# Four key tiles of the value product in parts, and two cosine products taken from PSUM by VectorE

## The chip, the cores and the metric

The kernel runs on one core of one Trainium2 chip. The metric is the device time in microseconds (us) of one execution, as the median of several runs; lower is better.

## The reference

A transformer block on four sequences of 1024 tokens with 256 channels: layer norm, then attention with 16 heads of 128 and rotary positions, and beside it a feed-forward net with weights rounded to four bits, both added to the input. All of it is computed in fp32.

```
xn = layernorm(x)
q, k, v = split(einsum('bsd,od->bso', xn, w_qkv))      # 16 heads of 128
q, k = x * cos + rotate_half(x) * sin                  # for each of the two
attn = softmax(q k^T / sqrt(128))                      # 1024 x 1024 for each head
x = x + (attn v) w_out^T + mxfp4_ffn(xn)
```

## The kernel before

**Tiling.** Attention takes the bulk of the time. It goes through 32 pairs of heads (8 pairs for each of four sequences). A pair is eight chunks of work, and a chunk is 256 query rows of one head against its 1024 keys. Chunks are numbered 0 to 7 within a pair here (0 to 15 within a round of two pairs, `k` in the code); `c` counts them through the whole run, 256 in all. There is one step of the program for each chunk. TensorE (PE) does in step k: the scores of the next chunk (two halves of a step, each a query tile of 128 rows against 1024 keys, six matmuls), the projection of a part of q, k or v for the next pair (the places `slot(0)` and `slot(1)`, not filled in every step), the output product of chunk k-2 (`output`, tile `w_ps`) and the value product of chunk k-1 (`values`, tile `o_ps`).

**Parts.** A product that must be exact is done either in fp32, or as three matmuls on numbers split in a high part (fp32r, the rounded copy) and a low part (the difference): high by high, high by low, low by high. The scores, the projections and the output product use parts. In the value product two of the eight key tiles are in parts (`SPLIT = 2`, lines 1296 to 1300) and six are in fp32 (line 1304).

**The way of a chunk.** ACT (ScalarE) turns scores into probabilities with an exponential (line 755) after DVE (VectorE) has found the row maxima (933). DVE transposes them in blocks (943, twice a chunk), the DMA queue of SyncE (SP) moves them to `keys_first` (420, eight DMAs a chunk), ACT makes the high parts of the split tiles (`probs_high`, 761, kept in `seq_parts`), GpSimd (POOL) makes the low parts (`probs_low`, 605), and PE multiplies. ACT (767) and DVE (963, `o_lo`) then split the result for the output product, and DVE adds that to `y` (974).

**Rotations.** Each pair has eight halves of q and k to rotate, m = 0 to 7: `qk0` has 0 to 3, `qk1` has 4 to 7. For each, ACT copies the projection from PSUM (735, and 736 and 737 for the two swapped halves; semaphore `rope_in`), POOL multiplies by cosine (584) and by sine (585) and adds (587; `rotated_sum`), ACT makes the high part (747, `rotated_high`) and POOL the low part (598, `rotated_low`). The buffers `rope_a` and `rope_b` hold two rotations, so the copy for m waits until the low part of m-2 is made.

**What sets the order.** No scheduler: each engine runs its own list in order, written in the functions called `step`. On ACT, `rotated_high` of m=0, 1, 2 stands at the end of steps 3, 4, 5, that of m=3 in the middle of step 6, those of m=4 and 5 at the end of steps 7 and 0, and `probs_high` comes last in each step. On POOL, `probs_low` of the chunk before comes first in each step, and the low part and the sum of the rotations after it. On SP, `move_tile` sends a half chunk once DVE has transposed it. In the first sequence POOL and ACT also split the weights of the next pair (612, 618, 705, 713); later these are loaded.

**Numbers that matter to the change.** `V_SPLIT` lists the v projections whose tiles get parts (`v_low` on DVE, 957). It follows from `SPLIT`.

## Time and profile before

| | us |
|---|---|
| median of 3 runs | 2454.54 (2453.13 to 2455.77) |
| the profiled execution | 2453.68 |
| its span | 2451.9 |
| PE busy | 2417.3 (99% of the span) |
| DVE busy | 1920.8 (78%) |
| POOL busy | 1731.7 (71%) |
| ACT busy | 1678.6 (68%) |

The span runs from the first to the last instruction; the profiled execution is 1.8 us longer than its span. The granted clock of TensorE is at 2.4 GHz throughout (0.999 of it on average). Busy time says how much work an engine has. Whether an engine that is not the busiest can still set the time is seen from the order of its work against that of the others, instruction by instruction.

### The profile page before, as it was taken

How to read it: one execution, taken by the hardware profiler on the slowest of the kernel's cores; microseconds unless marked ns; L12 is line 12 of the kernel's file. 1: busy time of each engine (PE TensorE's matmuls, PEld its weight loads, DVE VectorE, ACT ScalarE, POOL GpSimd, SP SyncE). 2: the span in 40 equal slices, each digit the busy share in tenths (PEclk: the TensorE clock that was granted, in tenths of full speed). 3: DMA queues.
4: the chain of work that ended last, by engine and by line, in shares of the span. 5: the costliest groups of instructions: out<-in, count | busy, mean ns of one | idle time of the engine just before them, and what ended most of it. 6: DMA issues, size and time to landing. Idle time of an engine off the chain costs nothing. (4 is left out here: it accounts for less than half of the span.)

```text
span 2451.9 us, 42811 instructions
## 1 busy us (share of the span) xinstructions
PE 2417.3 (99%) x13168; PEld 2123.8 (87%) x13168; DVE 1920.8 (78%) x2671; ACT 1678.6 (68%) x3039; POOL 1731.7 (71%) x1358
## 2 busy tenths in 40 slices
PE   6999999999999999999999999999999999999999
PEld 5888888888888888888888888888888888888798
DVE  7878888787877877787787778778777877777776
ACT  7777777776776777676677767667776766777433
POOL 4778877777777777777677777777777777777331
PEclk9999999999999999999999999999999999999999
DMA  4666666667666656667666666667676666656832
GB/s 143 181 170 167 169 158 177 158 167 195 183 161 150 156 148 162 156 151 195 180 159 147 164 154 152 162 149 190 158 183 156 151 162 149 156 146 171 240 132 69
DMA packets 400878, 396.72 MB, mean 162 GB/s; under 512 B 38656, under 2 KB 383104, under 8 KB 400768
## 3 DMA queue, kind: packets, MB, share of 16 engines
q1 hardware_dynamic: 400768, 395.67, 62.9%
q14 instruction: 91, 0.75, 0.1%
q8 instruction: 19, 0.31, 0.1%
HBM read 91.43 MB, written 35.65 MB: 52 GB/s over the span
## 5 line engine op out<-in xcount | busy, mean ns | idle before, releaser
L933 DVE TENSOR_REDUCE neg_max<-s_ps 128x1 f32<-128x1024 f32 x512 | 621.1, 1219 | 289.1 <-PE s_ps L1222 288.2
L1222 PE MATMUL s_ps<-seq_parts 128*128 128x512 f32 x3072 | 826.3, 408 | 1.3 <-DVE seq_parts L1097 0.8
L755 ACT ACTIVATE probs<-s_ps,neg_max 128x1024 f32<-128x1024 f32 x512 | 571.1, 1115 | 369.0 <-DVE neg_max L933 365.3
L1304 PE MATMUL o_ps<-keys_first,v_rows 128*128 128x256 f32 x3072 | 706.5, 380 | 1.3 <-ACT v_rows L722 1.3
L943 DVE STREAM_TRANSPOSE turned_blocks<-probs 128x1024 f32<-128x1024 f32 x512 | 630.6, 1237 | 61.3 <-ACT probs L755 38.8
L1222 PEld LDWEIGHTS s_ps<-seq_parts 128*128 128x128 f32 x3072 | 571.5, 188 | 116.9 <-ACT probs L755 1.4
L1304 PEld LDWEIGHTS o_ps<-keys_first,v_rows 128*128 128x128 f32 x3072 | 566.3, 190 | 68.1 <-ACT v_rows L722 1.5
L605 POOL TENSOR_TENSOR keys_first<-keys_first,seq_parts 128x512 fp32r<-128x512 f32 x256 | 333.0, 1301 | 318.1 <-ACT seq_parts L761 318.0
L584 POOL TENSOR_TENSOR rope_a<-rope_a,cos 128x512 f32<-128x512 f32 x252 | 325.7, 1292 | 178.8 <-ACT rope_b L737 178.6
L598 POOL TENSOR_TENSOR seq_parts<-rope_a,seq_parts 128x512 fp32r<-128x512 f32 x252 | 360.2, 1430 | 92.8 <-ACT seq_parts L747 92.8
L1222 PE MATMUL slot_ps<-seq_parts,w_parts 128*128 128x512 f32 x1506 | 387.9, 393 | 0.0
L587 POOL TENSOR_TENSOR rope_a<-rope_a,rope_b 128x512 f32<-128x512 f32 x252 | 326.0, 1294 | 19.8
L585 POOL TENSOR_TENSOR rope_b<-rope_b,sin 128x512 f32<-128x512 f32 x252 | 326.7, 1297 | 0.0
L1222 PEld LDWEIGHTS slot_ps<-seq_parts,w_parts 128*128 128x128 f32 x1506 | 272.9, 189 | 51.7 <-ACT rope_b L737 0.5
L747 ACT ACTIVATE seq_parts<-rope_a 128x512 fp32r<-128x512 f32 x252 | 222.1, 881 | 80.4 <-POOL rope_a L587 79.9
L974 DVE SCALAR_TENSOR_TENSOR y<-w_ps,inv_sum,y 128x256 f32<-128x256 f32 x512 | 224.4, 480 | 33.5 <-DVE inv_sum L951 7.8
L767 ACT ACTIVATE o_hi<-o_ps 128x256 fp32r<-128x256 f32 x256 | 98.0, 383 | 165.5 <-PE o_ps L1304 141.9
L1222 PEld LDWEIGHTS slot_ps<-w_parts,seq_parts 128*128 128x128 f32 x1524 | 197.5, 189 | 9.1 <-issue 0.9
L1222 PE MATMUL slot_ps<-w_parts,seq_parts 128*128 128x256 f32 x1524 | 203.1, 283 | 0.5 <-ACT rope_b L737 0.5
L1222 PEld LDWEIGHTS w_ps<-wo_parts,o_hi 128*128 128x128 f32 x1024 | 175.1, 190 | 29.5 <-DVE o_lo L963 9.1
L1222 PE MATMUL w_ps<-wo_parts,o_hi 128*128 128x256 f32 x1024 | 194.3, 282 | 6.4 <-DVE o_lo L963 6.3
L761 ACT ACTIVATE seq_parts<-keys_first 128x512 fp32r<-128x512 f32 x256 | 159.7, 624 | 59.3 <-DMA keys_first<-turned_blocks 57.8
(118 smaller groups left out, 2606.8 us busy)
## 6 DMA issues: line engine op xcount, KB each, us to landing
keys_first<-turned_blocks SPq DMA_DIRECT2D x2048, 128.0 KB, 2.7
w_parts<-w_qkv_parts SPq DMA_DIRECT2D x72, 512.0 KB, 4.2
w_qkv_parts<-w_parts SPq DMA_DIRECT2D x24, 512.0 KB, 3.7
wo_parts<-w_out_parts SPq DMA_DIRECT2D x48, 256.0 KB, 3.2
seq_parts<-xnt_parts SPq DMA_DIRECT2D x16, 512.0 KB, 4.4
w_raw<-in_w_qkv SPq DMA_DIRECT2D x24, 256.0 KB, 4.1
seq_parts<-xnt_parts SPq DMA_DIRECT2D x6, 1024.0 KB, 8.3
y<-in_x SPq DMA_DIRECT2D x16, 256.0 KB, 3.2
```

The lines of the kernel that those rows point to most:

```text
L584: nc.gpsimd.tensor_tensor(a, a, cos[:, cols], ALU.mult).then_inc(rope_mult, 1)
L585: nc.gpsimd.tensor_tensor(b, b, sin[:, cols], ALU.mult).then_inc(rope_mult, 1)
L587: nc.gpsimd.tensor_tensor(a, a, b, ALU.add).then_inc(rope_sum, 1)
L598: nc.gpsimd.tensor_tensor(lo, total, hi.bitcast(F32), ALU.subtract).then_inc(qk_ready, 1)
L605: nc.gpsimd.tensor_tensor(low, low.bitcast(F32), p_hi[:, slot, :, :, :].bitcast(F32), ALU.subtract).then_inc(p_lo_ready, 1)
L747: nc.scalar.activation(hi, total, ACT.Copy).then_inc(rope_hi, 1)
L755: nc.scalar.activation(probs[:, k2 % 4, :], s_ps[k2 % 2][:, :], ACT.Exp, bias=neg_max[:, col:col + 1], accum_out=row_sum[:, col:col + 1]). ...
L933: nc.vector.tensor_reduce(neg_max[:, k2 % 16:k2 % 16 + 1], s_ps[k2 % 2][:, :], AXX, ALU.max, negate=True).then_inc(max_ready, 1)
L943: nc.vector.transpose(turned_blocks[:, k % 2, n].rearrange("p b j q -> p j b q"), probs[:, (2 * k + n) % 4, :].rearrange("p (j b q) -> p j ...
L974: last = nc.vector.scalar_tensor_tensor(rows, w_ps[:, n * DIM:(n + 1) * DIM], inv_sum[:, col:col + 1], rows, ALU.mult, ALU.add)
L1222: ins = nc.tensor.matmul(out, w, m, start=(n == 0), stop=(n == len(terms) - 1))
L1304: last = nc.tensor.matmul(out, v_rows[:, parity, kt - SPLIT, cols], keys_first[:, slot, :, kt, :].bitcast(F32), start=False, stop=(kt == B ...
```

## The change

- `SPLIT` goes from 2 to 4: four key tiles of each value product are done in three fp32r matmuls each, four in fp32. The high parts of a chunk's probabilities are one ACT copy of 1024 columns in place of 512. The low parts are two POOL subtractions of 512 columns (`FRONT`, tiles 0 and 1; `BACK`, tiles 2 and 3), with a semaphore each, both waited for by PE before the low parts' matmuls. One more v projection in each pair gets a low part from DVE, in step 5.
- For m = 6 and 7 (`FROM_BANK`), ACT no longer copies the projection to `rope_a`, and POOL no longer multiplies it by the cosine: DVE takes it from PSUM, scales it and multiplies it by the cosine in one instruction (`rotated_product`). That stands in DVE's steps 0 (m=6) and 1 (m=7), behind the row maxima and ahead of the reciprocal, the sum to `y` and the transpose. It waits for ACT's two half copies (`rope_in`). POOL's sum and PE's next use of the bank wait for it.
- In step 2 POOL makes the low part of m=7 ahead of the low parts of chunk 1, and ACT its high part ahead of the exponentials.

```diff
-SPLIT = 2
+FRONT_TILES, SPLIT = 2, 4
...
+        FROM_BANK = (6, 7)
...
                 pool.wait_ge(rope_in, p * 8 + m + 1)
-                nc.gpsimd.tensor_tensor(a, a, cos[:, cols], ALU.mult).then_inc(rope_mult, 1)
+                if m in FROM_BANK:
+                    pool.wait_ge(rope_product, p * len(FROM_BANK) + FROM_BANK.index(m) + 1)
+                else:
+                    nc.gpsimd.tensor_tensor(a, a, cos[:, cols], ALU.mult).then_inc(rope_mult, 1)
...
-                low = keys_first[:, slot, :, 0:SPLIT, :]
-                nc.gpsimd.tensor_tensor(low, low.bitcast(F32), p_hi[:, slot, :, :, :].bitcast(F32),
-                                        ALU.subtract).then_inc(p_lo_ready, 1)
+                low = keys_first[:, slot, :, FRONT, :]
+                nc.gpsimd.tensor_tensor(low, low.bitcast(F32), p_hi[:, slot, :, FRONT, :].bitcast(F32),
+                                        ALU.subtract).then_inc(p_lo_front, 1)
+                low = keys_first[:, slot, :, BACK, :]
+                nc.gpsimd.tensor_tensor(low, low.bitcast(F32), p_hi[:, slot, :, BACK, :].bitcast(F32),
+                                        ALU.subtract).then_inc(p_lo_back, 1)
...
+                if k8 == 2:
+                    rotated_low(p, "qk1", 3)
                 if not (first and k == 0):
                     probs_low(c - 1, k - 1)
...
-                nc.scalar.activation(a, bank, ACT.Copy, scale=scale)
+                if m not in FROM_BANK:
+                    nc.scalar.activation(a, bank, ACT.Copy, scale=scale)
...
+            def rotated_product(p, part, n, bank):
+
+                m = qk_number(part, n)
+                half = qk_slot(part, n)[2]
+                dve.wait_ge(rope_in, p * 8 + m + 1)
+                nc.vector.scalar_tensor_tensor(rope_a[:, m % 2, :], bank, SCALE if n // 2 == 1 else 1.0,
+                                               cos[:, half * HALF:(half + 1) * HALF], ALU.mult, ALU.mult).then_inc(rope_product, 1)
...
-                pe.wait_ge(p_lo_ready, c + 1)
+                pe.wait_ge(p_lo_front, c + 1)
+                pe.wait_ge(p_lo_back, c + 1)
```

POOL in steps 1 and 2 of a pair, before (605 makes low parts of probabilities, 598 those of rotations):

```order
L605 TENSOR_TENSOR keys_first<-keys_first,seq_parts 128x8x64
L598 TENSOR_TENSOR seq_parts<-rope_a,seq_parts 128x512 x2
L583 REGISTER_ALU
L584 TENSOR_TENSOR rope_a<-rope_a,cos 128x512
L585 TENSOR_TENSOR rope_b<-rope_b,sin 128x512
L586 ISA
L587 TENSOR_TENSOR rope_a<-rope_a,rope_b 128x512
L603 REGISTER_ALU
L605 TENSOR_TENSOR keys_first<-keys_first,seq_parts 128x8x64
L598 TENSOR_TENSOR seq_parts<-rope_a,seq_parts 128x512
```

The same place in the changed kernel (619 and 622 are the two low parts of the probabilities, 612 those of the rotations, 599 the sine, 601 the sum):

```order
L619 TENSOR_TENSOR keys_first<-keys_first,seq_parts 128x8x64
L622 TENSOR_TENSOR keys_first<-keys_first,seq_parts 128x8x64
L612 TENSOR_TENSOR seq_parts<-rope_a,seq_parts 128x512 x2
L594 REGISTER_ALU
L596 REGISTER_ALU
L599 TENSOR_TENSOR rope_b<-rope_b,sin 128x512
L600 REGISTER_ALU
L601 TENSOR_TENSOR rope_a<-rope_a,rope_b 128x512
L612 TENSOR_TENSOR seq_parts<-rope_a,seq_parts 128x512
L617 REGISTER_ALU
L619 TENSOR_TENSOR keys_first<-keys_first,seq_parts 128x8x64
L622 TENSOR_TENSOR keys_first<-keys_first,seq_parts 128x8x64
```

Each chunk now has two subtractions, the cosine product of m=7 is gone, and its low part stands ahead of those of chunk 1.

DVE in step 1, before, from the transpose of chunk 1's second half to that of chunk 2's first half:

```order
L943 STREAM_TRANSPOSE turned_blocks<-probs 128x8x4x32
L963 TENSOR_TENSOR o_lo<-o_ps,o_hi 128x256
L932 REGISTER_ALU
L933 TENSOR_REDUCE neg_max<-s_ps 128x1
L932 REGISTER_ALU
L933 TENSOR_REDUCE neg_max<-s_ps 128x1
L951 RECIPROCAL inv_sum<-row_sum 128x2
L974 SCALAR_TENSOR_TENSOR y<-w_ps,inv_sum,y 128x256 x2
L939 ISA
L942 ISA
L943 STREAM_TRANSPOSE turned_blocks<-probs 128x8x4x32
```

And in the changed kernel (970 is the transpose):

```order
L970 STREAM_TRANSPOSE turned_blocks<-probs 128x8x4x32
L990 TENSOR_TENSOR o_lo<-o_ps,o_hi 128x256
L959 REGISTER_ALU
L960 TENSOR_REDUCE neg_max<-s_ps 128x1
L959 REGISTER_ALU
L960 TENSOR_REDUCE neg_max<-s_ps 128x1
L953 REGISTER_ALU
L954 SCALAR_TENSOR_TENSOR rope_a<-slot_ps,cos 128x512
L978 RECIPROCAL inv_sum<-row_sum 128x2
L1001 SCALAR_TENSOR_TENSOR y<-w_ps,inv_sum,y 128x256 x2
L966 ISA
L970 STREAM_TRANSPOSE turned_blocks<-probs 128x8x4x32
```

The product, with its wait, stands ahead of the transpose with which SP's moves of chunk 2 begin.

ACT at the end of a step that holds an `rotated_high`, before (747) and the copy of the high parts of the probabilities after it:

```order
L743 REGISTER_ALU
L747 ACTIVATE seq_parts<-rope_a 128x512
L760 ISA
L761 ACTIVATE seq_parts<-keys_first 128x512
L767 ACTIVATE o_hi<-o_ps 128x256
```

And in the changed kernel:

```order
L762 REGISTER_ALU
L766 ACTIVATE seq_parts<-rope_a 128x512
L780 ACTIVATE seq_parts<-keys_first 128x1024
L728 REGISTER_ALU
L730 ACTIVATE wo_parts<-wo_raw 128x256
L786 ACTIVATE o_hi<-o_ps 128x256
```

The order is the same; the copy is twice as wide.

## Rows read from the trace of the kernel before

**Rows 1.** The page, part 1: busy time of each engine.

```profile
PE 2417.3 (99%) x13168; PEld 2123.8 (87%) x13168; DVE 1920.8 (78%) x2671; ACT 1678.6 (68%) x3039; POOL 1731.7 (71%) x1358
```

**Rows 2.** Timeline of PE, value products: start, duration in us, line, tiles, count.

```profile
1201.28 0.29 PE L1296 MATMUL o_ps<-seq_parts,v_hi 128*128 128x256 f32 x1
1201.40 0.28 PE L1297 MATMUL o_ps<-seq_parts 128*128 128x256 f32 x1
...
1202.00 2.75 PE L1304 MATMUL o_ps<-keys_first,v_rows 128*128 128x256 f32 x12
...
1210.16 2.10 PE L1304 MATMUL o_ps<-keys_first,v_rows 128*128 128x256 f32 x9
```

**Rows 3.** Timeline of PE: chunk 7's value product starts, two pairs apart.

```profile
978.94 0.28 PE L1296 MATMUL o_ps<-seq_parts,v_hi 128*128 128x256 f32 x1
...
1121.77 0.28 PE L1296 MATMUL o_ps<-seq_parts,v_hi 128*128 128x256 f32 x1
```

**Rows 4.** Who waited for whom: total us, times, longest.

```profile
POOL keys_first L605 <- ACT seq_parts L761: 318.0, 181, 6.7
```

**Rows 5.** Timeline of POOL, steps 4 and 6: start, us, line, [idle before].

```profile
1006.94 1.30 POOL L605 TENSOR_TENSOR keys_first<-keys_first,seq_parts 128x512 fp32r<-128x512 f32 x1 [2.00 <-ACT seq_parts L761]
1008.19 1.55 POOL L598 TENSOR_TENSOR seq_parts<-rope_a,seq_parts 128x512 fp32r<-128x512 f32 x1
1009.70 1.29 POOL L584 TENSOR_TENSOR rope_a<-rope_a,cos 128x512 f32<-128x512 f32 x1
...
1012.33 1.30 POOL L587 TENSOR_TENSOR rope_a<-rope_a,rope_b 128x512 f32<-128x512 f32 x1
...
1024.54 1.29 POOL L605 TENSOR_TENSOR keys_first<-keys_first,seq_parts 128x512 fp32r<-128x512 f32 x1 [2.44 <-ACT seq_parts L761]
1025.79 1.30 POOL L598 TENSOR_TENSOR seq_parts<-rope_a,seq_parts 128x512 fp32r<-128x512 f32 x1
1027.04 1.30 POOL L584 TENSOR_TENSOR rope_a<-rope_a,cos 128x512 f32<-128x512 f32 x1
...
1029.67 1.29 POOL L587 TENSOR_TENSOR rope_a<-rope_a,rope_b 128x512 f32<-128x512 f32 x1
```

**Rows 6.** Timeline of ACT, ends of steps 3, 4 and 6.

```profile
1006.23 0.63 ACT L761 ACTIVATE seq_parts<-keys_first 128x512 fp32r<-128x512 f32 x1
...
1013.73 1.14 ACT L747 ACTIVATE seq_parts<-rope_a 128x512 fp32r<-128x512 f32 x1
1014.76 0.62 ACT L761 ACTIVATE seq_parts<-keys_first 128x512 fp32r<-128x512 f32 x1
...
1030.99 0.63 ACT L747 ACTIVATE seq_parts<-rope_a 128x512 fp32r<-128x512 f32 x1 [1.65 <-POOL rope_a L587]
1031.53 1.10 ACT L755 ACTIVATE probs<-s_ps,neg_max 128x1024 f32<-128x1024 f32 x1
...
1032.62 0.62 ACT L761 ACTIVATE seq_parts<-keys_first 128x512 fp32r<-128x512 f32 x1
```

**Rows 7.** Timelines of ACT and SP from step 1 to step 2.

```profile
989.40 0.59 ACT L737 ACTIVATE rope_b<-slot_ps 64x512 f32<-64x512 f32 x1
...
997.84 0.63 ACT L761 ACTIVATE seq_parts<-keys_first 128x512 fp32r<-128x512 f32 x1 [1.05 <-DMA keys_first<-turned_blocks]
...
990.76 5.08 SPq L420 DMA_DIRECT2D keys_first<-turned_blocks  x8
```

**Rows 8.** Timelines of DVE and PE from step 1 to step 2.

```profile
987.80 0.15 DVE L951 RECIPROCAL inv_sum<-row_sum 128x2 f32<-128x2 f32 x1
988.06 0.88 DVE L974 SCALAR_TENSOR_TENSOR y<-w_ps,inv_sum,y 128x256 f32<-128x256 f32 x2
988.85 1.24 DVE L943 STREAM_TRANSPOSE turned_blocks<-probs 128x1024 f32<-128x1024 f32 x1
...
992.42 0.39 DVE L963 TENSOR_TENSOR o_lo<-o_ps,o_hi 128x256 fp32r<-128x256 f32 x1
...
993.27 0.40 PE L1222 MATMUL w_ps<-wo_parts,o_hi 128*128 128x256 f32 x2
```

**Rows 9.** Instructions of one line, DVE's low part of v: nanoseconds least, median, most.

```profile
L957 DVE TENSOR_TENSOR seq_parts<-slot_ps,v_hi x31: 680/681/681, 107.8 to 2255.2; 128x512 fp32r<-128x512 f32 x31
```

29 lines of the change are left out of this document (20 added, 9 removed).

## The prediction

> **What bounds the kernel now.** I read the page's busy times first, then PE's timeline, then the list of waits, and last POOL, ACT and DVE side by side. PE is busy 99% of the span [rows 1], and in the steady part its steps follow one another without a gap: a pair of heads takes (1121.77 - 978.94) / 2 = 71.42 us [rows 3]. So the kernel is bound by PE's work. The one long wait between other engines is POOL's for ACT's high parts, 318.0 us [rows 4]. It costs nothing as long as PE doesn't feel it, but it shows a pattern that the change will load: POOL and ACT take turns.
>
> **The taking of turns.** Follow one turn from the end of the high-part copy of chunk 3, at 1006.23 + 0.63 = 1006.86 [rows 6]. POOL starts the low part 0.08 later, goes on to the low part of a rotation (1.25 after), then to the three operations of the next rotation (1.51 after), which end at 1012.33 + 1.30 = 1013.63, 3.93 after their start [rows 5]. ACT takes their sum 0.1 later, and the high-part copy of chunk 4 comes 1.03 after that and ends at 1015.38 [rows 6]. Nothing in this turn runs beside anything else in it: ACT's list has the copy of chunk 4 behind the rotation's high part, which needs POOL's sum, and POOL's list has that sum behind the low part of chunk 3. The turn takes 8.52 us. The turn from chunk 5 (its copy ends 0.08 before POOL's start at 1024.54, at 1024.46) to chunk 6 (1032.62 + 0.62 = 1033.24) takes 8.78 us, and its links sum to 0.08 + 1.25 + 1.25 + 3.92 + 0.03 + 0.54 + 1.09 + 0.62 = 8.78 [rows 5, 6], with no slack in it (an exponential stands ahead of the copy there). So two turns are already tight in themselves; others have slack, which is why the sum stays under 71.42.
>
> **The change on PE.** A fp32r matmul of 256 columns starts every 0.12 us; a fp32 tile is two records, and three records are worth 2.75 - 2.10 = 0.65 us, so a tile is 0.43 [rows 2]. A tile in parts is 3 x 0.12 = 0.36. Two tiles more in parts save 0.144 us a chunk, 1.15 a pair, 37 us in 256 chunks. PE alone would need 71.42 - 1.15 = 70.27 us a pair. The rule in the Trainium skill ("TensorE: Matmul & The Clock Gate", section "Back-to-back issue gap") is columns / 2.4 + 2.5 ns, an estimate of 109 ns for 256 columns. The row's 120 ns stands against it; by the rule the gain would be 512 x (0.43 - 3 x 0.109) = 53 us, and as hidden as the 37.
>
> **The change on the turns.** Per turn POOL gets a second subtraction, +1.25 (start to start [rows 5]), and ACT's copy goes from 512 to 1024 columns. No such copy is in the trace. Bounds: no fixed part falls away, 2 x 0.62 = 1.24, or only the start-to-start 0.52 (from 1013.73 + 1.03 and the like) counts twice, 1.04; the exponential of 1024 columns takes 1.10 [rows 6]. I take 1.15. New turns, each as: hand-over 0.08, low parts 2.50, low part of the rotation 1.51 (k half, strided) or 1.25, rotation 3.93, hand-over 0.03, high part 1.03 (strided) or 0.53, copy 1.15.
> - into chunk 4 and into chunk 0: 0.08 + 2.50 + 1.51 + 3.93 + 0.03 + 1.03 + 1.15 = 10.23 each
> - into 5: the same with the plain high part, 9.73
> - into 6: plain low part, plain high part, exponential 1.09 between: 0.08 + 2.50 + 1.25 + 3.93 + 0.03 + 0.54 + 1.09 + 1.15 = 10.57
> - into 7 and into 3: no low part of a rotation, 0.08 + 2.50 + 3.93 + 0.03 + 1.03 + 1.15 = 8.72 each.
>
> Sum of the six: 58.20 us.
>
> **From chunk 0 to chunk 2** the way is other, and DVE and SP are in it. Count from the end S of POOL's sum for m=5; chunk 0's copy ends at S + 0.03 + 1.03 + 1.15 = S + 2.21. POOL does sine and sum of m=6 (the cosine product is gone: 3.93 - 1.25 = 2.68, less an overlap of 0.09: next start at 2.59), two low parts of chunk 0 (5.09) and the low part of m=5 (ends 6.64). ACT's copy of m=7 waits for that buffer; it is now two half copies, 0.03 + 0.61 + 0.59 (the last is a row of [rows 7]), end 7.87. DVE's product waits for it. Its price isn't in the trace: nearest is the low part of v, 512 columns from PSUM with one operand in SBUF, 681 ns in each of 31 cases [rows 9], 0.60 to the next start; below, two of line 974 (0.80); above, 1.25 more if it had to wait out a POOL instruction. I take 0.08 + 0.60, and reach 8.55. The reciprocal, the two sums and the start of the transpose are 988.85 - 987.80 = 1.05, the transpose 1.24 [rows 8]: 10.84. SP then issues eight DMAs; from its first start to ACT's copy is 997.84 - 990.76 = 7.08 [rows 7]. The hand-over to SP is between 0 and 990.76 - 990.09 = 0.67; I take 0.30. The copy 1.15 ends at 19.37, less 2.21: 17.16 us from copy 0 to copy 2. In the kernel before, DVE did not wait for ACT here, which had the copies of m=7 done only at 989.99, when the transpose was already running.
>
> That product isn't slowed by POOL, I hold, since L957 varies by 1 ns over 31 cases with POOL at work beside most of them. The Trainium skill's "SBUF — State Buffer", section "Who interferes with whom", says the same of a DVE instruction with one SBUF input; on that only rival 4 hangs.
>
> **The sum.** The ring closes: 58.20 + 17.16 = 75.36 us a pair, against 70.27 that PE needs. PE has 5 us of idle time in each pair, and its own saving of 1.15 is lost in it. The period is 75.36 - 71.42 = 3.94 longer. Thirty pairs: 118.2. The first pair spends the slack that is there first, 2. In the first sequence POOL also has a split of weights (1.25) ahead of chunk 0's low parts, in seven pairs: 8.8. The others of its kind and wo's fall into POOL's waits for ACT (2.2 us a turn). The last pair has no rotations in six steps: -0.9. Sum 128. 2453.68 + 128 = 2581.7; the median shown is 0.9 above the profiled execution, so 2582.
>
> The other edits cost nothing in this: the further v low part on DVE (0.68 in step 5) delays row maxima that then wait for ACT anyway; the new order in step 2 only moves the low part of m=7, whose turn has 2 us of slack there while SP moves chunk 2. The feed-forward part doesn't change.
>
> **Range of the forecast.** Eight copies at 1.04 to 1.24: -0.9 to +0.7 a pair. SP's hand-over: -0.3 to +0.4. Together about 2545 to 2616.
>
> **Rivals.**
> 1. *PE's gain comes through*: no turn binds, 2453.7 - 37 + 0.9 = 2418. For it: POOL would be busy 16 x 1.25 + 22 x 1.3 + 8 x 1.4 = 60 of 70 us, ACT less. Against: the turn into 6 is tight before any load is added. 0.07.
> 2. *Gain eaten by the product alone*: the ring has slack I overlook, and only the late transposes of step 1 hurt. `o_lo` of chunk 0 ended at 992.81, and the output product began at 993.27 [rows 8], 0.46 of slack. DVE would end it 1.1 to 1.9 later, PE 0.3 earlier: a stall of 0.7 to 1.9, 1.3 on average against 1.15 saved. 32 x 0.15 = +5: 2459. It decides from a delay of 1.6 us on. 0.08.
> 3. *The ring closes but shorter*, since SP's moves of chunk 2 begin with an earlier event than the transpose, or the slack of some turn adds to the next. At 17.16 - 2 or so a pair takes 73.4: 2520; down to 2480. 0.14.
> 4. *Longer*: the product contends with POOL, or PE's late scores join the ring, 1.25 us or more a pair: 2620 to 2650. 0.06.
> The rest, 0.03, is for what I don't see; the forecast has 0.62.
>
> **How the numbers follow.** Range 2515 to 2618: the forecast's own and the upper half of rival 3; out of it fall rivals 1, 2, 4 and some of 3. A measurement of this kernel can tell 0.2%, 4.9 us, from no change. Faster: rival 1, 0.07. Same: half of rival 2 and little else, 0.05. Slower: the rest, 0.88.
>
> **What would show it.** PE's busy share at 95% or under and its value products starting about 75.4 us a pair apart. PE waiting mostly for `o_lo` of DVE, in steps 2 and 7 above all. Almost no idle time on POOL but for ACT's copy, on ACT but for POOL's sum, and turns of 9.7 to 10.6 us between copies from chunk 3 to 7. A copy of 1.15 us, a product of 0.68. A fp32r start every 0.12 us as before. If the turns from 3 to 6 come out near 9 us, the taking of turns was misread; if PE shows no waits, the whole forecast is wrong.

## The result, and the profile after

| | before | after |
|---|---|---|
| device time, median | 2454.91 us (4 runs, 2453.13 to 2455.77) | 2662.38 us (4 runs, 2659.65 to 2666.63) |
| ratio | 1 | 1.085, 95% interval 1.083 to 1.086 |
| profiled execution | 2453.68 us, span 2451.9 | 2663.94 us, span 2662.1 |
| TensorE's mean granted clock | 0.999 | 0.980 |

The change costs 207 us; 128 were forecast. The direction and the kind of loss were right, the size was not, and the time lies above the range. The page of the changed kernel, part 1, the row that answers to [rows 1]:

```profile
PE 2460.4 (92%) x13680; PEld 2145.2 (81%) x13680; DVE 1986.8 (75%) x2767; ACT 1756.4 (66%) x2975; POOL 1962.1 (74%) x1550
```

PE has fallen from 99% to 92% of its span, as forecast for a ring of waits that is longer than PE's work. But one number in this row doesn't fit the forecast: PE's busy time should have fallen by 37 us and has grown by 43. The mean clock of 0.980 accounts for the greater part: (1 - 0.980) x 2662, or some 50 us of full-speed time, are lost, and where they go comes back below. It isn't all. The four-tile kernels of the experiments that keep a clock of 0.995 to 0.997 still have PE busy for 2411 to 2429 us against 2417 before, so the 37 us don't show in the busy time. The ends of matmuls are modelled in these records, and no run here separates that from work.

The waits of the changed kernel that answer to [rows 4] (who waited for whom: total us, times, longest):

```profile
POOL keys_first L619 <- ACT seq_parts L780: 419.3, 185, 6.2
ACT probs L774 <- DVE neg_max L960: 372.4, 270, 5.7
ACT seq_parts L766 <- POOL rope_a L601: 267.0, 173, 4.1
...
PE s_ps L1253 <- POOL seq_parts L612: 99.8, 31, 3.5
...
DVE rope_a L954 <- ACT rope_b L756: 85.9, 48, 2.4
...
PE w_ps L1253 <- DVE o_lo L990: 40.9, 43, 2.7
```

POOL waits for ACT and ACT for POOL, as said. DVE's wait for ACT ahead of its new product was forecast too. PE's main wait was not. The prediction named `o_lo` of DVE; that is 40.9 us, and 99.8 us are waits for POOL's low part of a rotation, one in each of 31 pairs.

The turns are the measure. This table is worked out from the trace: the mean time between the ends of ACT's high-part copies of two successive chunks, over 30 pairs of heads, by the chunk into which the turn leads.

```
                 into 0    0 -> 2   into 3    4      5      6      7     sum
forecast          10.23    17.16     8.72   10.23   9.73  10.57   8.72   75.36
changed kernel    10.58    18.88     8.88   10.12   9.59  10.41   9.80   78.27
kernel before     10.80    16.28     8.30    9.15   8.73   8.80   9.52   71.58
```

Five of the seven entries are within 0.35 us of the forecast. Two are not: the turn into 7 (+1.08) and the way from copy 0 to copy 2 (+1.72). The first pair takes 6.4 us more than before (2 forecast), the last pair 3.2 more (0.9 less forecast), and what follows the last copy is as long as before.

**A turn as forecast.** POOL, timeline of the turn into chunk 6, the answer to [rows 5] (start, us, line, idle before):

```profile
1111.18 1.29 POOL L619 TENSOR_TENSOR keys_first<-keys_first,seq_parts 128x512 fp32r<-128x512 f32 x1 [1.69 <-ACT seq_parts L780]
1112.42 1.31 POOL L622 TENSOR_TENSOR keys_first<-keys_first,seq_parts 128x512 fp32r<-128x512 f32 x1
1113.67 1.31 POOL L612 TENSOR_TENSOR seq_parts<-rope_a,seq_parts 128x512 fp32r<-128x512 f32 x1
...
1117.52 1.26 POOL L601 TENSOR_TENSOR rope_a<-rope_a,rope_b 128x512 f32<-128x512 f32 x1
1119.52 1.27 POOL L612 TENSOR_TENSOR seq_parts<-rope_a,seq_parts 128x512 fp32r<-128x512 f32 x1 [0.74 <-ACT seq_parts L766]
```

and ACT's side, which answers to [rows 6]:

```profile
1110.06 1.04 ACT L780 ACTIVATE seq_parts<-keys_first 128x1024 fp32r<-128x1024 f32 x1
...
1118.82 0.63 ACT L766 ACTIVATE seq_parts<-rope_a 128x512 fp32r<-128x512 f32 x1 [4.13 <-POOL rope_a L601]
1119.35 1.10 ACT L774 ACTIVATE probs<-s_ps,neg_max 128x1024 f32<-128x1024 f32 x1
...
1120.44 1.04 ACT L780 ACTIVATE seq_parts<-keys_first 128x1024 fp32r<-128x1024 f32 x1
```

The copy of chunk 5 ends at 1111.10, POOL works without a gap from 1111.18 to 1118.78, ACT follows 0.04 later, and the copy of chunk 6 ends at 1121.48: 10.38 us, forecast 10.57. The copy of 1024 columns takes 1.05 us, the lower end of the bounds; I had taken 1.15.

**The turn into 7.** Next, the timeline of PE (start, us, line, tiles, count, wait before):

```profile
1120.93 2.90 PE L1253 MATMUL s_ps<-seq_parts 128*128 128x512 f32 x6 [3.52 <-POOL seq_parts L612]
1123.63 2.77 PE L1253 MATMUL slot_ps<-w_parts,seq_parts 128*128 128x256 f32 x12
1126.20 1.95 PE L1253 MATMUL s_ps<-seq_parts 128*128 128x512 f32 x6
1127.98 0.40 PE L1253 MATMUL w_ps<-wo_parts,o_hi 128*128 128x256 f32 x2
```

and the same stretch by windows (us, busy time and records of PE, PEld, DVE, ACT, POOL, then PE's granted clock, DMA share, GB/s):

```profile
1113.00:1118.00 5.00, 4.42 (x26) 3.64 (x24) 3.19 (x5) 1.68 (x3) 4.92 (x5) 1.00 0.58 168
1118.00:1120.90 2.90, 0.00 (x0) 0.00 (x0) 0.33 (x1) 2.08 (x4) 2.05 (x2) 0.88 0.63 143
1120.90:1124.00 3.10, 3.06 (x8) 2.54 (x9) 1.44 (x3) 2.52 (x5) 2.44 (x2) 0.50 0.38 85
1124.00:1126.00 2.00, 2.00 (x12) 2.00 (x11) 1.10 (x1) 0.87 (x1) 2.00 (x3) 0.50 0.75 184
1126.00:1128.00 2.00, 2.00 (x9) 1.64 (x9) 0.00 (x0) 0.93 (x3) 1.83 (x2) 0.74 0.00 2
```

This is one of three pairs in which the clock stays low longest. The scores of a new pair's first head need the fourth rotation, so PE waits for its low part (L612, ending 1120.79). In this pair the clock falls from 2.4 to 1.2 GHz 0.7 us before PE starts again. Over the 25 pairs in which it falls, it does so between 0.9 us before that start and 1.5 us after it, so often not in the wait but just behind it. The work that follows runs at half speed. In the kernel before the same six matmuls take 1.73 us:

```profile
972.53 1.73 PE L1222 MATMUL s_ps<-seq_parts 128*128 128x512 f32 x6
974.10 1.54 PE L1222 MATMUL slot_ps<-seq_parts,w_parts 128*128 128x512 f32 x6
975.48 1.52 PE L1222 MATMUL s_ps<-seq_parts 128*128 128x512 f32 x6
```

Behind PE stand the row maximum, the second exponential, and, behind that in ACT's list, the copy of chunk 7 (ACT):

```profile
1129.44 1.12 ACT L774 ACTIVATE probs<-s_ps,neg_max 128x1024 f32<-128x1024 f32 x1 [2.41 <-DVE neg_max L960]
...
1130.55 1.14 ACT L766 ACTIVATE seq_parts<-rope_a 128x512 fp32r<-128x512 f32 x1
1131.58 1.06 ACT L780 ACTIVATE seq_parts<-keys_first 128x1024 fp32r<-128x1024 f32 x1
```

POOL's sum, which in my reckoning sets this turn, had ended at 1127.90. The turns into 7 fall into three groups, which follow the clock. In one the clock stays at 2.4 GHz, the way from the first scores to the output product takes 4.3 us and the turn 8.62 to 8.64: five of the 30 pairs, and 8.72 was forecast. In 22 that way takes 5.6 to 5.8 and the turn 9.7 to 10.0; in three, 7.0 and 11.1. So POOL's and ACT's part of this turn was reckoned rightly, and what is missing is the fall of the clock. The full-speed time lost in this turn (one less the granted clock, times the time, summed over 30 pairs) is 42 us.

**The turn into 0.** It takes 10.13 us in 17 pairs and 11.15 in the other 13, each the first pair of a round. There DVE's list has instructions of the feed-forward net's rounding (`mx_amax`, lines 1058 and 1060, 1.2 us each) ahead of a transpose and of the row maxima of step 0, and ACT's two exponentials wait for these. DVE, then ACT:

```profile
1134.05 1.22 DVE L1060 TENSOR_SCALAR mx_amax<-mx_amax 128x8 uint32<-128x8 uint32 x1
...
1138.14 1.12 ACT L774 ACTIVATE probs<-s_ps,neg_max 128x1024 f32<-128x1024 f32 x1 [2.60 <-DVE neg_max L960]
...
1140.59 1.12 ACT L774 ACTIVATE probs<-s_ps,neg_max 128x1024 f32<-128x1024 f32 x1
```

POOL's sum ends at 1140.62, but the second exponential has just begun and stands ahead of the high part and the copy: 1.1 us more. In the 17 other pairs the second exponential has ended before POOL's sum. In two first pairs of a round `mx_amax` ends 1.2 us sooner, and the turn takes 10.13 there too. No run moved these instructions, so the cause is read from the traces and not tested.

**From copy 0 to copy 2.** The rows are of a pair with the longer turn into 0. DVE in step 1, which answers to [rows 8]:

```profile
1145.43 1.25 DVE L970 STREAM_TRANSPOSE turned_blocks<-probs 128x1024 f32<-128x1024 f32 x1
...
1146.91 2.34 DVE L960 TENSOR_REDUCE neg_max<-s_ps 128x1 f32<-128x1024 f32 x2
1151.61 0.69 DVE L954 SCALAR_TENSOR_TENSOR rope_a<-slot_ps,cos 128x512 f32<-128x512 f32 x1 [2.36 <-ACT rope_b L756]
...
1152.46 0.88 DVE L1001 SCALAR_TENSOR_TENSOR y<-w_ps,inv_sum,y 128x256 f32<-128x256 f32 x2
1153.26 2.36 DVE L970 STREAM_TRANSPOSE turned_blocks<-probs 128x1024 f32<-128x1024 f32 x2
```

ACT in the same step, which answers to [rows 7]:

```profile
1142.75 1.04 ACT L780 ACTIVATE seq_parts<-keys_first 128x1024 fp32r<-128x1024 f32 x1
...
1148.15 1.12 ACT L774 ACTIVATE probs<-s_ps,neg_max 128x1024 f32<-128x1024 f32 x1 [3.29 <-DVE neg_max L960]
...
1150.38 0.59 ACT L755 ACTIVATE rope_b<-slot_ps 64x512 f32<-64x512 f32 x1
1150.99 0.59 ACT L756 ACTIVATE rope_b<-slot_ps 64x512 f32<-64x512 f32 x1
```

Counted from S, the end of POOL's sum for m=5 (1140.62), the low part of m=5 ends at S + 7.41 (1148.03) where I had 6.64: POOL waits 0.75 for DVE's other product, that of m=6. Then ACT should take the copy of m=7 at once, but its list has an exponential, a copy of v and a rotated high part ahead of it, and that exponential waits for a row maximum that DVE made only at 1148.11. The copies end at S + 10.96 and not 7.87, the first transpose at S + 13.87 and not 10.84. SP then takes 7.20 (7.38 forecast). Copy 0 itself ends 0.97 later than reckoned, behind an exponential, which takes a part back. In the pairs between, POOL doesn't wait for the product, copy 0 ends as reckoned, and the copies of m=7 end at S + 9.3: still 1.4 late, behind the same instructions of ACT's list. In the mean of 30 pairs the copies end at S + 10.06 and the first transpose at S + 12.98.

### The profile page after: what moved, and what is told of

It reads as the page before. It is cut to its first block and busy times, and to the rows that moved or that the text cites. A ratio compares the mean times of both kernels' runs of the same rounds, so it can differ in the third digit from the quotient of the medians.

```text
span 2662.1 us, 44562 instructions
## 1 busy us (share of the span) xinstructions
PE 2460.4 (92%) x13680; PEld 2145.2 (81%) x13680; DVE 1986.8 (75%) x2767; ACT 1756.4 (66%) x2975; POOL 1962.1 (74%) x1550
## 5 line engine op out<-in xcount | busy, mean ns | idle before, releaser
L1253 PE MATMUL s_ps<-seq_parts 128*128 128x512 f32 x3072 | 847.2, 416 | 112.7 <-POOL seq_parts L612 99.8
L1253 PEld LDWEIGHTS s_ps<-seq_parts 128*128 128x128 f32 x3072 | 584.1, 194 | 244.6 <-ACT probs L774 112.8
L960 DVE TENSOR_REDUCE neg_max<-s_ps 128x1 f32<-128x1024 f32 x512 | 613.8, 1217 | 184.0 <-PE s_ps L1253 180.9
L619 POOL TENSOR_TENSOR keys_first<-keys_first,seq_parts 128x512 fp32r<-128x512 f32 x256 | 332.8, 1300 | 419.9 <-ACT seq_parts L780 419.3
L1339 PE MATMUL o_ps<-keys_first,v_rows 128*128 128x256 f32 x2048 | 487.2, 381 | 9.4 <-ACT v_rows L740 9.4
L612 POOL TENSOR_TENSOR seq_parts<-rope_a,seq_parts 128x512 fp32r<-128x512 f32 x252 | 355.9, 1412 | 99.4 <-ACT seq_parts L766 99.4
L1339 PEld LDWEIGHTS o_ps<-keys_first,v_rows 128*128 128x128 f32 x2048 | 371.2, 190 | 53.0 <-ACT v_rows L740 12.7
L601 POOL TENSOR_TENSOR rope_a<-rope_a,rope_b 128x512 f32<-128x512 f32 x252 | 327.1, 1298 | 19.8
L780 ACT ACTIVATE seq_parts<-keys_first 128x1024 fp32r<-128x1024 f32 x256 | 268.9, 1050 | 98.0 <-DMA keys_first<-turned_blocks 97.9
L622 POOL TENSOR_TENSOR keys_first<-keys_first,seq_parts 128x512 fp32r<-128x512 f32 x256 | 330.1, 1290 | 0.0
L1330 PE MATMUL o_ps<-seq_parts,v_hi 128*128 128x256 f32 x1024 | 259.6, 286 | 0.0
L1331 PE MATMUL o_ps<-seq_parts 128*128 128x256 f32 x1024 | 258.0, 285 | 0.0
L598 POOL TENSOR_TENSOR rope_a<-rope_a,cos 128x512 f32<-128x512 f32 x188 | 242.6, 1290 | 18.9 <-ACT rope_b L756 18.9
L1253 PE MATMUL w_ps<-wo_parts,o_hi 128*128 128x256 f32 x1024 | 200.4, 288 | 41.5 <-DVE o_lo L990 40.9
```

The source lines that it names most:

```text
L601: nc.gpsimd.tensor_tensor(a, a, b, ALU.add).then_inc(rope_sum, 1)
L612: nc.gpsimd.tensor_tensor(lo, total, hi.bitcast(F32), ALU.subtract).then_inc(qk_ready, 1)
L619: nc.gpsimd.tensor_tensor(low, low.bitcast(F32), p_hi[:, slot, :, FRONT, :].bitcast(F32), ALU.subtract).then_inc(p_lo_front, 1)
L622: nc.gpsimd.tensor_tensor(low, low.bitcast(F32), p_hi[:, slot, :, BACK, :].bitcast(F32), ALU.subtract).then_inc(p_lo_back, 1)
L780: nc.scalar.activation(p_hi[:, k % 2], keys_first[:, k % 2, :, 0:SPLIT, :].bitcast(F32), ACT.Copy).then_inc(p_hi_ready, 1)
L960: nc.vector.tensor_reduce(neg_max[:, k2 % 16:k2 % 16 + 1], s_ps[k2 % 2][:, :], AXX, ALU.max, negate=True).then_inc(max_ready, 1)
```

## The experiments

Times are medians, each ratio to runs of the kernel before on the same chip.

### What is the cost made of: product, second subtraction, order

**Without the product** (four tiles stay in parts):

```diff
-        FROM_BANK = (6, 7)
+        FROM_BANK = ()
```

> The changed kernel with the two cosine products given back to ACT (copy) and POOL (multiplication); four tiles stay in parts, the order of step 2 stays. Theory T (the turns of POOL and ACT, closed to a ring, set the time): the turns from chunk 2 to chunk 0 are untouched by this edit, 58 to 59 us a pair as now, and only the way from chunk 0 to chunk 2 changes (two cosine products of 1.25 more on POOL, no product on DVE): 16 to 19 us. So the time stays within 2590 to 2680 us. Rival P (the product on DVE, with its wait ahead of the transpose, is the cost): most of the 208 us comes back, 2420 to 2480 us.

Measured: 2684.7 us, ratio 1.093 (1.091 to 1.096), 5 us over theory T's range and far from rival P's. With four tiles the product is no cost, it saves 22 us. The way from copy 0 to 2 is shorter without it (16.56 against 18.88), but the turn into 3 takes 12.18 instead of 8.88, and PE's clock falls there as well (36 us of full-speed time in this turn). That turn theory T had as untouched.

**Two tiles, with product and new order:**

```diff
-FRONT_TILES, SPLIT = 2, 4
+FRONT_TILES, SPLIT = 2, 2
...
-                low = keys_first[:, slot, :, BACK, :]
-                nc.gpsimd.tensor_tensor(low, low.bitcast(F32), p_hi[:, slot, :, BACK, :].bitcast(F32),
-                                        ALU.subtract).then_inc(p_lo_back, 1)
...
-                pe.wait_ge(p_lo_back, c + 1)
```

> Two tiles in parts as before, with one subtraction and a copy of 512 columns per chunk, but the two cosine products on DVE and the new order in step 2 as in the changed kernel. Theory T: the turns have their old length (8.5 and 8.8 us where tight), so PE sets the pace but for a stall of 0.7 to 1.9 us a pair in step 2, where DVE's product delays o_lo: 2470 to 2515 us. Rival P: nearly the whole loss, 2600 us or more. If the product is harmless: 2455.

Measured: 2503.3 us, 1.020 (1.017 to 1.022), as theory T said. Two tiles more in parts are worth 159 of the 207 us.

**Four tiles, POOL's second subtraction gone** (the last two pieces of the diff above, and not the first; this kernel leaves out the low parts of tiles 2 and 3, and PE multiplies their full values instead):

> The changed kernel without the second subtraction (BACK) on POOL and without PE's wait for it: the low parts of tiles 2 and 3 are left out (the full values are multiplied in their place). PE's matmuls, ACT's copy of 1024 columns and the products on DVE are as in the changed kernel. Theory T: each of eight turns is 1.25 us shorter, 78.4 - 10 = 68.4 us, under the 70.3 that PE needs, so PE sets the pace again but for stalls of 1 to 2 us a pair: 2420 to 2480 us. Rival L (PE itself is slowed, or the wider copy or the product costs the time): 2600 us or more.

Measured: 2508.7 us, 1.022 (1.020 to 1.024). One instruction of 1.25 us in each turn carries 154 us. The time is still 29 us over theory T's range: the way from copy 0 to copy 2 takes 19.20 us here, no less than in the changed kernel. The mean clock is 0.997 and no turn into 7 has a fallen one: 8.52 us in the mean.

**The new order of step 2 alone, the product alone**, each with two tiles; and the changed kernel with the old order (the diff, against the changed kernel, takes the new order back; it is in the last two of the three kernels, and ACT's `rotated_high(p, "qk1", 3)` moves likewise):

```diff
-                if k8 == 2:
-                    rotated_low(p, "qk1", 3)
                 if not (first and k == 0):
                     probs_low(c - 1, k - 1)
...
+                if k8 == 2:
+                    rotated_low(p, "qk1", 3)
```

> Two tiles in parts as in the kernel before, no product on DVE: only the new order of step 2 is left (POOL makes the rotation's low part ahead of the chunk's, ACT the rotated high part ahead of the first exponential). The same with the product took 2503 us, the kernel before 2455. Theory O (the order costs, since the first exponential of step 2 and the chunk's low part wait behind the rotation, and the product helps a little as it did with four tiles): 2500 to 2530 us, with the step into the second value product about 2 us longer than before. Rival P (the product on DVE costs the 48 us, since it stands ahead of the inverse and the transposes on DVE and waits for POOL's port): 2450 to 2465 us.

> The kernel before with DVE's cosine products alone: two tiles in parts, step 2 in the old order. With the new order too it took 2503 us, the new order alone 2495 us, the kernel before 2455 us. Theory A (the parts add up): the product costs 8 us, 2460 to 2468 us. Rival H (without the order's stall the product's relief of ACT and POOL shows): 2435 to 2452 us, TensorE being busy 99% of 2452. Rival D (DVE's product in step 1 delays the transposes and with them the copy of chunk 2, which the order hid): 2470 to 2500 us.

> The changed kernel with the order of step 2 as it was before (POOL: chunk's low parts, then the rotation's; ACT: first exponential, then the rotated high part). With two tiles in parts the new order alone cost 40 us. Theory O (the new order costs here too, since the first exponential of step 2 stands behind a rotated high part that waits for POOL): 2600 to 2650 us. Rival N (with four tiles the steps around it are bound by the ring and the order is worth nothing): 2655 to 2670 us. Rival H (with four tiles the order helps, since the rotation's low part no longer waits for 2.5 us of subtractions): 2675 to 2710 us.

Measured: the order alone 2495.3 us, 1.016 (1.014 to 1.018); the product alone 2503.8, 1.019 (1.018 to 1.021); the old order in the changed kernel 2663.2, 1.085 (1.083 to 1.087). With two tiles either costs 40 to 48 us, and both together no more than one (2503.3), so the parts don't add up; with four, the order is worth nothing (rival N). The prediction had priced it at nothing, which holds in the changed kernel, but only because other waits hide it: with a shorter ring the old order is worth 12 us (the last section of experiments). In the order-alone kernel PE itself waits for the chunk's low part:

```profile
PE o_ps L1331 <- POOL keys_first L619: 39.2, 32, 3.1
```

### The ring

**The copy ahead of the rotated high part** at the end of steps 3, 4, 5, 7 and 0:

```diff
+                    probs_high(i, k)
                     if k % 8 == 3 and more_pairs:
                         rotated_high(p + 1, "qk0", 0)
...
-                    probs_high(i, k)
```

> The changed kernel with ACT's copy of the high parts of the probabilities (probs_high) ahead of rotated_high at the ends of steps 3, 4, 5, 7 and 0, in place of behind it. No work is added or taken away. Theory T: POOL finds the copy ready when it ends a rotation and doesn't wait for two ACT instructions between; the ring is open, and a pair takes what PE needs with stalls of 1 to 3 us, 71 to 73.5: 2430 to 2520 us. Rival L (the sheer load on POOL, 1962 us busy, or contention): no change, 2640 to 2680 us.

Measured: 2606.2 us, 1.060 (1.058 to 1.063). It is neither theory T nor rival L. 56 us come back, much less than the theory said: the turns into 3, 4 and 7 shorten by 0.7, 1.7 and 2.0, but that into 5 grows by 0.6, that into 6 stays, since its exponential and high part still stand ahead of the copy, and the way from 0 to 2 grows by 1.6.

**POOL's rotation low part first** in steps 0, 1, 4, 5 and 6, so that it runs beside ACT's copy; in the changed kernel and in the kernel before:

```diff
+                if k8 == 6 and more_pairs:
+                    rotated_low(p + 1, "qk0", 2)
                 if not (first and k == 0):
                     probs_low(c - 1, k - 1)
...
                 if k8 == 6 and more_pairs:
-                    rotated_low(p + 1, "qk0", 2)
                     rotated_sum(p + 1, "qk0", 3)
```

> The changed kernel (2662 us); POOL makes the rotation's low part at the start of steps 0, 1, 4, 5 and 6 ahead of the chunk's two subtractions instead of behind them, so that it runs beside ACT's copy of the chunk. Theory T (the ring of turns sets the time in steps 4 to 6, and everything in it counts): the turns into 4, 5 and 6 lose the 1.05 us that the copy takes, 3.2 us in each of 31 pairs, 2540 to 2580 us, and down to 2500 if the turns into 0 and 1 lose it too. Rival S (the second chain, from the fourth piece's low part over TensorE's late scores to the copy of chunk 0, takes back what the ring gives): turns into 4 to 6 shorter, those into 7 and 0 longer, 2630 to 2670 us. Rival C (POOL isn't free that early, so the order changes nothing): 2655 to 2670 us.

> The kernel before (2455 us) with POOL's rotation low part first at the start of steps 0, 1, 4, 5 and 6, nothing else. Theory T (with two tiles in parts the turns of 8.4 to 9.6 us wait for TensorE, not the other way round, so a shorter ring gives nothing): 2450 to 2458 us. Rival S (the ring held the 1 us that a pair took over TensorE's own work, 71.4 against 70.3 us): 2420 to 2440 us. Rival L (the chunk's low part comes later and the value product waits for it): 2465 to 2500 us.

Measured: 2607.8 us, 1.063 (1.061 to 1.065); in the kernel before 2454.7, 1.000 (0.999 to 1.001). In the changed kernel that lies between theory T's range and rival S's: turns of the ring shorten, others give a part back. The turns into 4 and 6 lose 1.0 us each, as the ring says, that into 5 0.3, that into 7 1.1, and those from 7 to 2 grow by 1.4 together. PE's wait for the low part is still there, but shorter, and the clock never falls in these 30 pairs:

```profile
PE s_ps L1258 <- POOL seq_parts L612: 34.4, 27, 2.2
```

In the kernel before the order is worth nothing, so two tiles leave the ring slack.

**The subtraction moved to DVE**, and that with the copy first:

```diff
+                if not (first and k == 0) and not (tail and k > 16):
+                    dve.wait_ge(p_hi_ready, c)
+                    low = keys_first[:, (k - 1) % 2, :, BACK, :]
+                    nc.vector.tensor_tensor(low, low.bitcast(F32), p_hi[:, (k - 1) % 2, :, BACK, :].bitcast(F32),
+                                            ALU.subtract).then_inc(p_lo_back, 1)
```

> The changed kernel with the low part of tiles 2 and 3 (512 elements a partition) taken from POOL and given to DVE, between the second row maximum and the rest of the step; what is computed stays the same. Theory T (POOL's second subtraction, 1.25 us in each turn of the ring, is what makes the ring longer than TensorE's work): about the time of the kernel without that subtraction, 2509 us, plus what DVE's share costs, 2500 to 2560 us, with turns of 8.0 to 9.0 us into steps 4 to 7. Rival D (DVE, 75% busy, takes over as the late engine, since a subtraction of two SBUF operands waits for POOL up to 1.4 us and the inverse, the addition and the next transposes stand behind it): 2590 to 2680 us.

> As the kernel with the subtraction of tiles 2 and 3 on DVE, and at the end of steps 3, 4, 5, 7 and 0 ACT copies the chunk's high part ahead of the rotated one, so that the ring loses the rotated high part and POOL has its next work sooner. Theory T (the ring is the sum of what stands in it; without the second subtraction and the rotated high part it is 6.9 to 8.0 us a turn, shorter than TensorE's 8.8): TensorE sets the time, with the rest lost in steps 0 to 2: 2425 to 2490 us. Rival D (DVE becomes the late engine): 2520 to 2620 us. Rival Q (the copy waits for its data where it stands early, so the order gives nothing once the ring is short): within 15 us of the version without the reordering.

Measured: 2632.0 us, 1.071 (1.069 to 1.073), and 2637.3, 1.074 (1.071 to 1.077). Against the kernel without the subtraction, DVE's share costs 123 us: rival D. The second kernel is 17 us over rival D's range and 5 from the first, as rival Q said. The turns into 5, 6 and 7 shorten (to 9.16, 9.53 and 8.47), that into 4 doesn't (10.08). The instruction takes 0.67 to 1.83 us, and behind it stand other engines' waits:

```profile
L1185 DVE TENSOR_TENSOR keys_first<-keys_first,seq_parts x256: 665/870/1825, 56.9 to 2508.6; 128x512 fp32r<-128x512 f32 x128
...
  PE o_ps L1337: 50.9, 64
```

### The turn into 7

**In step 7 the second exponential behind the copy:**

```diff
-                    if not (last and k == 15):
+                    if not (last and k == 15) and k % 8 != 7:
                         exponentials(t + 3, 2 * k + 3, first and k == 0)
...
                     probs_high(i, k)
+                    if not (last and k == 15) and k % 8 == 7:
+                        exponentials(t + 3, 2 * k + 3, first and k == 0)
```

> The changed kernel (2662 us) with one edit: in step 7 ACT makes the rotated high part of the fifth piece and the high part of the chunk's four tiles ahead of the step's second exponential instead of behind it. Theory J (a second chain joins the ring in step 7: TensorE's first scores of the new head wait 3.2 us for POOL's low part of the fourth piece, so the second row maximum and its exponential come 1.2 us after POOL's sum has ended, and the copy stands behind them): the turn into step 7 falls from 9.9 to 8.1 to 8.7 us, 1.2 to 1.8 us less in each of 31 pairs, 2605 to 2628 us. Rival R (the turn is long because POOL's own work is, the exponential's lateness only shows it): the turn stays at 9.7 to 10 us and the time at 2655 to 2670. Rival G (given back: the later exponential holds the next step's scores): the turn into 7 falls, that into 0 or 1 grows by as much, 2650 to 2680.

Measured: 2677.5 us, 1.090 (1.089 to 1.092). Rival G. The turn into 7 falls from 9.80 to 8.58, that into 0 grows from 10.58 to 11.75: the exponential is needed itself, for the transposes of chunk 0. So it is no help to step past PE's late scores: they reach two copies.

**Only chunk 5's second subtraction left out**, and with it PE's wait for it (the low parts of two tiles are left out of the result there):

```diff
-                low = keys_first[:, slot, :, BACK, :]
-                nc.gpsimd.tensor_tensor(low, low.bitcast(F32), p_hi[:, slot, :, BACK, :].bitcast(F32),
-                                        ALU.subtract).then_inc(p_lo_back, 1)
+                if k % 8 != 5:
+                    low = keys_first[:, slot, :, BACK, :]
+                    nc.gpsimd.tensor_tensor(low, low.bitcast(F32), p_hi[:, slot, :, BACK, :].bitcast(F32),
+                                            ALU.subtract).then_inc(p_lo_back, 1)
```

> The changed kernel without POOL's second subtraction in chunk 5 of each pair alone (the low part of its tiles 2 and 3 is left out of the result), so that POOL's low part of the fourth piece, for which TensorE's first scores of the next head wait, comes 1.25 us sooner; nothing else moves. Theory J (that low part, over the scores, the row maxima and the exponentials, sets the copies of chunk 7 and of chunk 0): the turn into 6 falls by 1.25 us and those into 7 and 0 don't grow, 1.25 us x 31 = 39 us less, 2610 to 2630 us. Rival G (the way to copy 7 or 0 is set by something that doesn't start with POOL's step 6, so the gain is given back there): 2652 to 2665 us.

Measured: 2610.1 us, 1.062 (1.059 to 1.065). Theory J, and more: 52 us for an instruction that takes 1.25 us in each of 32 pairs, 40 us. The turn into 6 loses its 1.25, and that into 7 another 0.54, since the clock falls in 15 of 30 pairs instead of 25 (25 us of full-speed time there instead of 42). PE's wait has shortened, to 2.0 to 2.3 us in the pairs in which the clock falls:

```profile
PE s_ps L1254 <- POOL seq_parts L612: 54.8, 31, 2.3
```

### From copy 0 to copy 2

**DVE's product behind the addition**: in the changed kernel, in the kernel with the product alone, and together with POOL's low part first.

```diff
-                for n, taken in ((1, g_before), (0, g)):
-                    if taken and taken[1] != "v" and qk_number(taken[1], taken[2]) in FROM_BANK:
-                        rotated_product(i * 2 + taken[3], taken[1], taken[2], slot_ps[:, n])
                 if has_out:
                     invert(c - 2, 2 * k - 4)
                     add_out(c - 2, (k - 2) % 16, (i // 4) if k >= 2 else ((i - 1) // 4))
+                for n, taken in ((1, g_before), (0, g)):
+                    if taken and taken[1] != "v" and qk_number(taken[1], taken[2]) in FROM_BANK:
+                        rotated_product(i * 2 + taken[3], taken[1], taken[2], slot_ps[:, n])
```

> The changed kernel (2662 us); DVE makes its product behind the inverse and the addition of the step instead of ahead of them. In steps 0 and 1 DVE stood idle for 1.37 and 2.36 us for ACT's last copy out of PSUM, with the addition (1.1 us) and the transposes behind it. Theory W (this in-order wait delays the transposes of chunk 2 and with them the copy of chunk 2): the addition fills the wait, the transposes come 1.0 us sooner and the product no later; the way from copy 0 to copy 2 falls from 19.0 to 18.0 us or less, 31 us less, 2600 to 2635 us. Rival N (the way is set by something else, such as ACT's exponentials): 2655 to 2668 us.

> The kernel before with the product alone (2504 us with the product ahead of the addition), the product now behind the inverse and the addition. Theory W: the 2 us that the second value product's step lost a pair are DVE's wait for ACT; one of them comes back, 31 us, 2465 to 2480 us. Rival N (POOL's rotation or its low part of chunk 1 comes late whatever DVE does): 2498 to 2510 us.

> The changed kernel with both orders: POOL's rotation low part first (2608 us alone) and DVE's product behind the addition. Theory W with T (the losses of steps 4 to 7 and of steps 0 to 2 lie one behind the other): what the product's place gives alone comes off 2608 too, 2555 to 2590 us. Rival M (they overlap, since PE waits once for either): 2600 to 2612 us.

Measured: 2627.2 us, 1.071 (1.068 to 1.074); 2453.4, 0.999 (0.998 to 1.000); 2547.5, 1.038 (1.036 to 1.040). Theory W each time, and twice by more than it said: with two tiles the product's whole 48 us are gone, 12 us under the range, and with both orders the time is 8 us under it. DVE with two tiles, first with the product ahead (timeline, steps 0 and 1):

```profile
1145.56 0.69 DVE L951 SCALAR_TENSOR_TENSOR rope_a<-slot_ps,cos 128x512 f32<-128x512 f32 x1 [0.20 <-ACT rope_b L753]
...
1156.98 0.69 DVE L951 SCALAR_TENSOR_TENSOR rope_a<-slot_ps,cos 128x512 f32<-128x512 f32 x1 [2.01 <-ACT rope_b L753]
...
1157.85 0.88 DVE L998 SCALAR_TENSOR_TENSOR y<-w_ps,inv_sum,y 128x256 f32<-128x256 f32 x2
1158.64 2.36 DVE L967 STREAM_TRANSPOSE turned_blocks<-probs 128x1024 f32<-128x1024 f32 x2
```

then behind the addition:

```profile
1121.67 0.68 DVE L951 SCALAR_TENSOR_TENSOR rope_a<-slot_ps,cos 128x512 f32<-128x512 f32 x1
...
1130.51 0.88 DVE L998 SCALAR_TENSOR_TENSOR y<-w_ps,inv_sum,y 128x256 f32<-128x256 f32 x2
1131.72 0.69 DVE L951 SCALAR_TENSOR_TENSOR rope_a<-slot_ps,cos 128x512 f32<-128x512 f32 x1 [0.33 <-ACT rope_b L753]
1132.33 2.36 DVE L967 STREAM_TRANSPOSE turned_blocks<-probs 128x1024 f32<-128x1024 f32 x2
```

From the first product to the transposes of step 1 it is 13.08 us ahead and 10.66 behind; about 1 us of that is only that the first product has itself moved behind an addition. The addition of step 1 now lies in the wait, and what stands ahead of it comes sooner too. In the mean of 30 pairs the way from copy 0 to copy 2 falls from 19.22 to 17.26 us. In the changed kernel the way from 0 to 2 falls from 18.88 to 17.36, but the turn into 3 gives 0.6 back. Both orders together take 115 us off, where their single gains (35 and 55) add up to 90. So the losses lie one behind the other, and more: low part first alone lengthens the way from 0 to 2 by 0.78, and with the product behind the addition it no longer does (17.07).

### Towards a kernel that beats both

> The changed kernel with POOL's rotation low part first, DVE's product behind the addition (2547.5 us together) and step 2 in the order of before. Theory O (the value products into steps 2 and 3 now wait 1.6 us a pair for POOL's second low part, because the new order of step 2 puts the rotation's low part ahead of it): a part of it comes back, 2500 to 2535 us. Rival N (the wait only moves to the turn into step 3, since POOL's work there is the same in sum): 2540 to 2555 us. Neither expects it under the 2455 us of before: the turns of this kernel add up to 74.6 us, TensorE's work there to 70.3.

> As the run before this one, and at the end of step 3 ACT copies the chunk ahead of the first piece's rotated high part, so that the turn into step 3 (8.7 to 10.2 us) loses that part and its wait for POOL. Theory T (the ring holds it): 0.6 us or more in each of 31 pairs, 15 to 35 us under the run before. Rival Q (the copy waits for its data anyway, or the time comes back in the turn into step 4): within 8 us of it.

The edits are those shown above, put together. Measured: 2535.5 us, 1.033 (1.031 to 1.035), and 2541.6, 1.036 (1.031 to 1.040). The old order of step 2 gives 12 us here, at the upper edge of theory O. With the copy first in step 3 the turn into 3 falls from 8.85 to 7.64 and that into 4 grows from 9.20 to 11.18, rival Q; the two times can't be told apart. The best four-tile kernel is 80 us over the kernel before. Its ring takes 74.0 us a pair. With two tiles the best is 2453.4, which these measurements can't tell from before.

## Why the forecast was wrong

**Right.** That a ring of turns between POOL and ACT binds once POOL has a second subtraction (without it, 154 us are gone); the length of the turns into 3, 4, 5 and 6, within 0.2 us of the means; PE's 0.12 us from start to start and its 92% of the span; the product's 0.69 us, which POOL doesn't disturb (680 to 694 ns in 64 cases; 0.68 assumed). The rule of the Trainium skill on this ("SBUF — State Buffer", section "Who interferes with whom") holds for the product with its one SBUF operand; the subtraction moved to DVE, with two SBUF operands, spreads from 665 to 1825 ns, and the section says of such an instruction that it contends with a GpSimd instruction that reads SBUF.

**Wrong, by 80 us (2662 against 2582).** The step that failed is the same in the three terms that were too short: the sums go from POOL's sum straight on to ACT's next instruction ("hand-over 0.03, high part 1.03 (strided) or 0.53, copy 1.15"), as if ACT stood ready. On ACT's list an exponential stands ahead of it, which waits for a row maximum of DVE. Only the turn into 6 had its exponential in the sum; the turns into 3, 4 and 5 came out within 0.2 us of the forecast without it. The kernel before showed the danger in the very turn that was read out, into 4, where the exponential ends 0.1 us after POOL's sum:

```profile
1012.62 1.12 ACT L755 ACTIVATE probs<-s_ps,neg_max 128x1024 f32<-128x1024 f32 x1
```

1. *Into 7, 8.72.* With a clock of 2.4 GHz the exponential is through in time and the turn is 8.63. What failed besides is that PE's idle time was taken as free of cost ("PE has 5 us of idle time in each pair, and its own saving of 1.15 is lost in it"). 3.2 us of it in the mean stand in one piece ahead of the new head's scores, and in 25 of 30 pairs the clock falls towards its end or just behind it. The work behind runs at 1.2 GHz and delays the exponential that stands ahead of the copy. +1.08 in the mean, 32 us in 30 pairs. Rival 4 named it ("PE's late scores join the ring") and got 0.06.
2. *Copy 0 to copy 2, 17.16.* The step that failed is "ACT's copy of m=7 waits for that buffer; ... end 7.87". ACT stood at an exponential that waits for a row maximum (S + 7.5 in the pair shown, behind a transpose), and it had a copy of v and a rotated high part to do first. +1.72, 52 us. Moving the product by two instructions takes 1.5 of it back.
3. *Into 0, 10.23*, measured 10.58: the exponential again, late in 13 of 30 pairs. 10 us.

The turns into 4 to 6 were 0.1 to 0.2 shorter each, mainly the copy's 1.05 instead of 1.15 (-12 us), and that into 3 0.16 longer (+5). This gives +87. The first and the last pair add 4 each. Against them stand 9 us that had been set apart for splits of weights and lie in the turns already, 5 because a pair took 71.58 us before in the mean and not 71.42, and about 2 because the profiled execution lies 1.6 us above the median. That is the 80.

Of the edits held to cost nothing, the order of step 2 cost nothing in this kernel, though 40 us with two tiles. Rival 2's price was real, 48 us or 1.5 a pair for the product alone with two tiles, but its mechanism only in part: of PE's waits there 19.1 us are for `o_lo`, as it says, and 19.8 for ACT's copy of v.

## To carry to other kernels

When two in-order engines hand work to each other, write the turn out as a sum. It came out to 0.2 us where it named what ended last, and was 0.35 to 1.7 us short in the mean where an instruction queued ahead waited for a third engine. Then look where TensorE's new idle time will stand. In the kernel with the low part first PE idles 4.3 us a pair in pieces of at most 2.2 us, and the clock stays; in the changed kernel a piece of 3.2 us in the mean was followed by half speed in 25 of 30 pairs. An instruction that waits belongs behind those that don't depend on it: two lines exchanged were worth 50 us with two tiles, 35 with four.

## What the hardware showed that I had not expected

- TensorE's clock was at half speed in 25 of 30 pairs after a wait of 2.7 to 3.5 us, and stayed at full speed in the other five after waits of 1.9 to 3.5; in the kernel with the low part first, with waits of up to 2.2 us, it never fell there, but without chunk 5's second subtraction it fell in 15 of 30 pairs after waits of 2.0 to 2.3. So the length of the wait alone doesn't tell whether it falls. A fall cost 1.7 us of full-speed time, or twice that. The Trainium skill ("TensorE: Matmul & The Clock Gate", section "What's actually happening") has the low state as the default, out of which activity brings the array; the trace agrees in so far as the clock shows 0.50 after a wait and comes back while PE works, in the windows above between 1126 and 1128.
- Moving one instruction to another engine isn't neutral: the subtraction takes 1.29 us on POOL and 0.67 to 1.83 on DVE, where it made the kernel 123 us slower than leaving it out.
- ACT's copy of 1024 columns takes 1.05 us against 0.62 for 512, so the second half costs 0.43.
